# New orders for the attention steps of a transformer block with adaptive layer norms and a mixture of experts

## What is computed

```python
h = _layernorm(x, axis=-1) * (1 + ca) + sa
x = x + ga * _L0_attn_ref(h, ...)   # inner layer norm, k, v, r, running sum over rows, Wo
h = _layernorm(x, axis=-1) * (1 + cb) + sb
x = x + gb * _L0_ffn_ref(h, ...)    # two groups of 32 experts, top 2 of each, SwiGLU
```

## Time and profile before

| what | value |
|---|---|
| time, median of 3 runs | 4911.22 us (4901.27 to 4916.95) |
| time of the profiled execution | 4905.73 us |
| its span | 4904.0 us |
| TensorE busy | 4580.8 us (93%) |
| VectorE busy | 3080.2 us (63%) |
| GpSimd busy | 2858.1 us (58%) |
| ScalarE busy | 1651.2 us (34%) |
| mean granted clock of TensorE | 0.971 |

### The profile page before, as it was taken

One profiled execution on the slowest core, in us unless ns is written; L12 is line 12 of the kernel. 1 busy time (PEld: TensorE's weight loads), 2 busy tenths in 40 slices (PEclk: granted clock), 3 DMA queues, 4 the chain that ended last, 5 costly groups with the idle time before them and its releaser, 6 DMA issues.

```text
span 4904.0 us, 89177 instructions
## 1 busy us (share of the span) xinstructions
PE 4580.8 (93%) x22649; PEld 3764.6 (77%) x22649; DVE 3080.2 (63%) x6077; ACT 1651.2 (34%) x4093; POOL 2858.1 (58%) x2300
## 2 busy tenths in 40 slices
PE   6999999999999995889999998999999999999998
PEld 4877777777777774667777777888788888888887
DVE  5999999999999996444444444444344444444443
ACT  2444444444444442222222222332222222222222
POOL 2577777777777776445444454555455555555554
PEclk8999999999999997899999999999999999999999
DMA  6767666666666674889899989998998988988887
GB/s 240 234 200 228 195 222 196 214 200 220 207 200 227 196 226 159 261 271 285 252 279 280 280 238 270 294 278 223 290 239 222 260 221 242 258 231 221 220 222 195
DMA packets 434624, 1152.46 MB, mean 235 GB/s; under 512 B 59361, under 2 KB 59362, under 8 KB 415666
## 3 DMA queue, kind: packets, MB, share of 16 engines
q0 software_dynamic: 182512, 454.27, 39.3%
q1 hardware_dynamic: 231106, 619.79, 36.6%
q10 hardware_dynamic: 20736, 75.51, 4.2%
HBM read 719.35 MB, written 463.57 MB: 241 GB/s over the span
## 4 chain that ended last, share of the span: by engine, by line
PE 42%; DMA 12%; issue 4%; POOL 2%; DVE 1%; POOLq 0%; SPq 0%; ACT 0%; DVEq 0%
PE ps L1316 12%; PE ps L1318 12%; PE ps L1317 12%; DMA out<-c_yo,c_idx 11%; PE ps L1325 4%; PE ps L1344 2%; POOL out L1307 1%; POOL c_xg L1274 1%; DMA c_wt<-wsp_d 0%; POOLq L1299 0%; DVE c_yo L1571 0%; POOL list_d L1279 0%; DMA list_d<-pairs,sidx 0%; DMA c_lists<-list_d,c_rowu 0%; DVE c_xl L1559 0%
## 5 line engine op out<-in xcount | busy, mean ns | idle before, releaser
L1307 POOL DMA_INDIRECT out<-c_yo,c_idx x576 | 915.1, 1589 | 933.9 <-DMA out<-c_yo,c_idx 512.5
L1316 PE MATMUL ps<-c_wt,c_xh 128*128 128x512 f32 x2304 | 964.1, 418 | 24.9 <-issue 16.8
L1318 PE MATMUL ps<-c_wt,c_xl 128*128 128x512 f32 x2304 | 910.3, 395 | 0.0
L1317 PE MATMUL ps<-c_wt,c_xh 128*128 128x512 f32 x2304 | 904.0, 392 | 0.0
L1274 POOL DMA_INDIRECT c_xg<-h2g_d,c_idx x576 | 565.0, 981 | 507.6 <-DVE c_yo L1571 400.5
L1555 DVE TENSOR_TENSOR c_hh<-ps,c_sil 128x256 f32<-128x256 f32 x576 | 244.2, 424 | 913.5 <-ACT c_sil L1398 843.5
L1571 DVE SCALAR_TENSOR_TENSOR c_yo<-ps,c_wc,c_xg 128x512 f32<-128x512 f32 x576 | 432.3, 750 | 529.2 <-PE ps L1318 261.5
L442 PE MATMUL ps<-xTh,wTh 128*128 128x512 f32 x1536 | 625.9, 407 | 53.5 <-DVE xTl L818 46.9
L1403 ACT CAST c_xh<-ps 128x512 fp32r<-128x512 f32 x576 | 339.2, 589 | 962.2 <-PE ps L1325 874.2
L709 POOL DMA_INDIRECT list_d<-pairs,sidx x496 | 545.5, 1100 | 188.5 <-issue 123.9
L1398 ACT ACTIVATE c_sil<-ps 128x256 f32<-128x256 f32 x576 | 221.3, 384 | 1177.1 <-PE ps L1318 1105.3
(11 more groups left out here) (199 smaller groups left out, 7776.2 us busy)
## 6 DMA issues: line engine op xcount, KB each, us to landing
c_wt<-wsp_d SPq DMA_DIRECT2D x69, 2048.0 KB
sraw<-wex SPq DMA_DIRECT2D x290, 256.0 KB
wsp_d<-shigh SPq DMA_DIRECT2D x288, 256.0 KB
wsp_d<-sraw SPq DMA_DIRECT2D x288, 256.0 KB
c_wt<-wsp_d SPq DMA_DIRECT2D x69, 1024.0 KB
xin<-x SPq DMA_DIRECT2D x34, 1024.0 KB
h2g_d<-mod_d SPq DMA_DIRECT2D x128, 256.0 KB
out<-xin SPq DMA_DIRECT2D x32, 1024.0 KB
```

Source lines behind the costliest of these rows:

```text
L1307: nc.gpsimd.indirect_dma_start(out=out, out_offset=bass.IndirectOffsetOnAxis(ap=idx[:, n:n + 1], axis=0), in_=yo[:, n % 4, :], in_offset=N ...
L1316: nc.tensor.matmul(o, lh, rh, start=first, stop=False)
L1317: nc.tensor.matmul(o, lh, rl, start=False, stop=False)
L1318: return nc.tensor.matmul(o, ll, rh, start=False, stop=last)
```

## The change

The order of work inside a step is new on all five engines. TensorE puts `back` after the k part of chunk 3, and `logits` behind `front`, at the end of the step; the group numbers follow, so that some groups take their bank from other groups than before. ScalarE takes jobs 0 and 1 ahead of chunk 0, `hi` of chunk 0 ahead of `soften`, jobs 4 to 6 earlier, and the logits' copy and job 9 last. GpSimd spreads the last five indirect DMAs over the step's start and moves jobs 7 and 9. VectorE takes chunk 0 ahead of `topk`, job 4 ahead of `modulate`, and jobs 5 and 6 ahead of chunk 1. SyncE issues `store_h2` after the store of job 4 instead of before it. In three places a `tensor_scalar` that adds EPS to the variances becomes a `tensor_reduce` that sums each variance and an EPS kept beside it.

The group numbers, and SyncE's queue:

```diff
-PROJ = ((0, 1, 2), (8, 9, 10), (11, 12, 13), (18, 20, 21))
-OUTP, RANK, BACKT, LOGIT, FRONTT = 3, 7, 14, 19, 22
+PROJ = ((0, 1, 2), (8, 9, 10), (11, 12, 13), (14, 19, 20))
+OUTP, RANK, BACKT, FRONTT, LOGIT = 3, 7, 15, 21, 25
...
                 turn(4)
                 if not (first and s == 0):
                     store_x1(b, s - 1)
+                turn(5)
+                if not (first and s == 0):
                     store_h2(b, s - 1)
...
-                for i in range(5, PER_STEP):
+                for i in range(6, PER_STEP):
                     turn(i)
```

TensorE:

```diff
                 project(b, s, 1)
                 project(b, s, 2)
+                project(b, s, 3, (0,))
                 if not (first and s == 0):
                     back(b, s)
-                project(b, s, 3, (0,))
+                project(b, s, 3, (1, 2))
+                front(b, s)
                 if not (first and s == 0):
                     logits(b, s)
-                project(b, s, 3, (1, 2))
-                front(b, s)
```

ScalarE:

```diff
-                chunk_k(b, s, 0)
                 stage_hi(b, at)
                 stage_hi(b, at + 1)
+                chunk_k(b, s, 0)
                 chunk_r(b, s, 0)
+                hi(b, s, 0)
                 if not (first and s < 2):
                     soften(b, s - 2)
-                hi(b, s, 0)
                 stage_hi(b, at + 2)
                 stage_hi(b, at + 3)
+                stage_hi(b, at + 4)
                 normed(b, s)
-                stage_hi(b, at + 4)
+                stage_hi(b, at + 5)
                 chunk_k(b, s, 1)
-                stage_hi(b, at + 5)
+                stage_hi(b, at + 6)
                 chunk_r(b, s, 1)
                 chunk_k(b, s, 2)
+                hi(b, s, 1)
                 if back_too:
                     turned(b, s)
-                hi(b, s, 1)
-                stage_hi(b, at + 6)
                 chunk_r(b, s, 2)
                 chunk_k(b, s, 3)
                 hi(b, s, 2)
                 stage_hi(b, at + 7)
-                if back_too:
-                    logits(b, s)
                 stage_hi(b, at + 8)
-                stage_hi(b, at + 9)
                 front(b, s, (0, 1))
                 chunk_r(b, s, 3)
                 front(b, s, (2, 3))
                 hi(b, s, 3)
+                if back_too:
+                    logits(b, s)
+                stage_hi(b, at + 9)
```

GpSimd:

```diff
+                stage_lo(b, at)
+                if not (first and s < 3):
+                    scatter(b, s - 3, 11, 13)
                 rstd(f_var, vaf, h_ready, rsf, f_rstd, b, s + 1)
+                stage_lo(b, at + 1)
+                receive(b, s, 0)
                 if not (first and s < 3):
-                    scatter(b, s - 3, 11, 16)
-                stage_lo(b, at)
-                receive(b, s, 0)
-                stage_lo(b, at + 1)
+                    scatter(b, s - 3, 13, 14)
                 lo(b, s, 0)
+                if not (first and s < 3):
+                    scatter(b, s - 3, 14, 16)
+                stage_lo(b, at + 2)
                 rstd(g_var, vag, z_ready, rsg, g_rstd, b, s + 1)
-                stage_lo(b, at + 2)
                 stage_lo(b, at + 3)
...
                 receive(b, s, 2)
-                if old:
-                    scatter(b, s - 2, 8, 9)
+                stage_lo(b, at + 7)
                 lo(b, s, 2)
-                stage_lo(b, at + 7)
                 stage_lo(b, at + 8)
...
-                stage_lo(b, at + 9)
                 receive(b, s, 3)
                 if old:
                     scatter(b, s - 2, 10, 11)
                 lo(b, s, 3)
+                stage_lo(b, at + 9)
```

VectorE (of the three edits of the EPS one is shown, and not the memory of three values a row that they read, nor its filling at the start):

```diff
-                    V.tensor_scalar(vaf[:], mvf[:, :, 1], EPS, None, ALU.add).then_inc(f_var, 1)
+                    V.tensor_reduce(vaf[:], mvf[:, :, 1:3], AX_X, ALU.add).then_inc(f_var, 1)
...
                 norm_front(b, s + 1, 1)
+                chunk(b, s, 0)
                 if not (first and s < 2):
                     topk(b, s - 2)
-                chunk(b, s, 0)
                 norm_front(b, s + 1, 2)
                 if not (first and s == 0):
                     residual(b, s - 1)
                 norm_front(b, s + 1, 3)
                 if not (first and s < 2):
                     place(b, s - 2)
+                stage_lo(b, s * PER_STEP + 4)
                 if not (first and s == 0):
                     modulate(b, s - 1)
-                stage_lo(b, s * PER_STEP + 4)
+                stage_lo(b, s * PER_STEP + 5)
+                stage_lo(b, s * PER_STEP + 6)
                 chunk(b, s, 1)
-                stage_lo(b, s * PER_STEP + 5)
                 chunk(b, s, 2)
-                stage_lo(b, s * PER_STEP + 6)
                 norm_front(b, s + 2, 0)
```

More of the change, by code:

```diff
@@ L284, in worked @@
             if n < 0:
-                return n == -1 and q >= FRONTT
+                return n == -1 and FRONTT <= q < FRONTT + KC
             behind = 2 if q == RANK else 1 if OUTP <= q < RANK or BACKT <= q < BACKT + KC or q == LOGIT else 0
@@ L803, in norm_front @@
                              (g_var, cnt(b, s - 1, 1, 1)), (g_nm, cnt(b, s - 1, 1, 1)))
-                        V.bn_aggr(mvg[:, j, :], stg[:, j, :]).then_inc(g_aggr, 1)
+                        V.bn_aggr(mvg[:, j, 0:2], stg[:, j, :]).then_inc(g_aggr, 1)
                     dve.wait_ge(g_aggr, cnt(b, s, 4, 4))
                     wait(dve, g_rstd, cnt(b, s - 1, 1, 1))
-                    V.tensor_scalar(vag[:], mvg[:, :, 1], EPS, None, ALU.add).then_inc(g_var, 1)
+                    V.tensor_reduce(vag[:], mvg[:, :, 1:3], AX_X, ALU.add).then_inc(g_var, 1)
                 else:
@@ L855, in residual @@
                          (b_var, cnt(b, s - 1, 1, 1)), (h2_half, cnt(b, s - 1, 4, 4)))
-                    V.bn_aggr(mvb[:, j, :], stb[:, j, :]).then_inc(b_aggr, 1)
+                    V.bn_aggr(mvb[:, j, 0:2], stb[:, j, :]).then_inc(b_aggr, 1)
                 dve.wait_ge(b_aggr, cnt(b, s, 4, 4))
                 wait(dve, b_rstd, cnt(b, s - 1, 1, 1))
-                V.tensor_scalar(vab[:], mvb[:, :, 1], EPS, None, ALU.add).then_inc(b_var, 1)
+                V.tensor_reduce(vab[:], mvb[:, :, 1:3], AX_X, ALU.add).then_inc(b_var, 1)
             def modulate(b, s):
@@ L1036, in _ @@
             g.memset(half[:], -0.5)
+            for t in (A["mvf"], A["mvg"], A["mvb"]):
+                g.memset(t[:, :, 2:3], EPS)
             g.memset(hit[:], 0.0)
```

12 lines of the change are left out of this document (6 added, 6 removed).

## The result

| | before | changed |
|---|---|---|
| time, median | 4906.25 us (4901.12 to 4916.95, 4 runs) | 5034.84 us (5030.85 to 5046.68, 4 runs) |
| ratio to before, 95% interval | | 1.0263 (1.0236 to 1.0290) |
| profiled execution, its span | 4905.73, 4904.0 us | 5032.62, 5030.9 us |
| mean granted clock of TensorE | 0.971 | 0.951 |

The change is 2.6% slower, by 129 us. The direction was the forecast's, the size was not: 5035 lies above 4936 and outside 4850 to 5010. It is close to the rival that called the DMA queue the decider (5020).

A forecast was written before the change was run, and what follows sets the result against it. Neither TensorE nor VectorE alone bounds the kernel; they wait for each other in turn. The new chain takes 58.0 us a step against 57.1, 25 us more over 28 steps, giving 4936 us, range 4850 to 5010.

The forecast's parts named there:

- the rival that called the DMA queue the decider: Slower rival: later landing of job 2's and job 4's stores plus TensorE's clock drop, 61 us a step, 5020; chance 0.20.
- the chain: Stage A step: outputs at +20.0, through stores and job 6 to chunk 3's scan at +52.9, next step at 58.0 us.
- The landing: SyncE's queue: job 4's store behind the 1 MB of x lands 8.1 us after the store of x, at +38.6.
- TensorE gets idle time near +42 and before v of chunk 3, both hidden behind VectorE's chain: TensorE late in the step: two idle times said to move at no cost to the step's length.
- The sum: Whole kernel: 0.9 us a step, 25 us over the loop's 28 steps, batch 0's four steps left unchanged; 4936 us.
- `soften`: ScalarE: running after the wait for outputs instead of hidden in it puts 3.95 us on the path, the change's cost.
- gain (1): TensorE at the step's start: `logits` covers the copies and `split_x`, removing a gap worth up to 1.0 to 3.3 us.
- Gain (2): VectorE: fewer collisions with GpSimd at L795 and job 6 free 2.5 and 2.2 us a step.
- Gain (3): VectorE: the 1044 ns `tensor_scalar` becomes a reduction of 0.2 us, freeing some 0.8 us a step; two alike count nothing.
- Faster: the stores are never late: Rival: job 4's store lands by +36, VectorE has no stall, 55.2 us a step, 4858 us; chance 0.27.
- Much faster: Rival: TensorE alone bounds, as `soften` and weight jobs find cover; 52.75 us a step, 4788 us; chance 0.05.
- nothing: Rival: engines wait for each other and slack only changes places, within 15 us of 4911; chance 0.06.

The follow-up runs named there:

- experiment 5: Changed kernel with job 6 moved back on VectorE (behind chunks 1 and 2) and ScalarE (behind the copies of h's transposes): 5028.97 us, 1.0259.
- experiment 3: Changed kernel with `soften` put back ahead of `hi` of chunk 0 on ScalarE: 5019.84 us, 1.0233.
- experiment 14: Changed kernel with the five moves of experiment 8, and group numbers 18 (chunk 3's first group) and 14 to 17 (h's transposes): 4926.27 us, 1.0023.
- experiment 2: Changed kernel with the 1 MB store of x moved behind job 4's store on SyncE's queue: 4959.83 us, 1.0102.
- experiment 12: Changed kernel with two group numbers altered (18 for chunk 3's first group, 14 to 17 for h's transposes): 5027.70 us, 1.0242.
- Experiment 13: Changed kernel with job 6 back on both engines (experiment 5) and the two group numbers of experiment 11: 4931.27 us, 1.0030.
- experiment 7: Kernel before with only TensorE's new order and group numbers, plus the logits' copy and job 9 last, which this forces: 5051.25 us, 1.0309.
- 8: Changed kernel with job 6 back on both engines, x's store behind job 4's, `soften` ahead of `hi`, GpSimd's norm power first: 5070.05 us, 1.0347.
- 9: Changed kernel with TensorE's old order and group numbers, the logits' copy and job 9 as before: 5060.51 us, 1.0302.
- 15: Changed kernel with TensorE's old order and numbers, and job 6 moved back on both engines: 4999.73 us, 1.0175.
- experiment 11: Kernel before with TensorE's new order as in experiment 7, but numbers 18 for chunk 3's first group and 14 to 17 for h's transposes: 4889.41 us, 0.9954.
- 6: Changed kernel with `topk` ahead of chunk 0 on VectorE again: 5024.02 us, 1.0258.

## Why the prediction was wrong

**Up to the middle of the step the chain held** (offsets in the changed step that begins at 1159.82). `hi` of chunk 0 was forecast at +20.0 and came at +19.8 (1179.61); the low part of job 2 was to end at +26.4 and ended at +26.2 (1186.03); `place` was to end at +30.2 and was done when job 4's low part began, at +31.0 (1190.79); the store of x was due at +30.5 and issued at +30.8, that of job 4 at +31.5 against +31.8. VectorE's stall before job 6 was forecast as 2 us and is 3.17.

**The landing was undersized.** Job 6's low part was to be done by +39.9; VectorE went on at 1201.16, +41.3, so 1.4 us are missing. Of these 1.2 are the landing: I took 8.1 us from the store of x to ScalarE's going on, and it was 9.27 (1190.63 to 1199.90). The rest is the store's later issue.

**The step that failed** is the sentence "TensorE gets idle time near +42 and before v of chunk 3, both hidden behind VectorE's chain". The place and the releaser of the idle time were right. Hidden it was not: the clock fell to the 1.2 GHz level behind it. At full clock the 12 transposes take 1.53 us (experiment 5) and not 2.82, and the eleven next gaps between starts are 0.23 us and not 0.43: 3.5 us more. The first 1.3 us, of the transposes, were slack, since v of chunk 3 had to wait for the scan of chunk 2 until 1207.64 in any case. The 2.2 us behind it were not: VectorE's own wait for v of chunk 3, 1.91 us, is what came through. 58.0 plus 1.4 plus 1.9 is 61.3, against 61.1 measured.

The trace of the changed kernel also has steps with the wait and without the slow clock. In the one from 425.35 to 483.63 TensorE waited 3.73 us in `back`, but the clock was high again for v of chunk 3:

```profile
472.33 0.50 PE L444 MATMUL ps<-xTh,wTh 128*128 128x512 f32 x1 [0.76 <-DVE cs L841]
472.66 0.40 PE L445 MATMUL ps<-xTl,wTh 128*128 128x512 f32 x1
```

VectorE didn't wait for it there, and the step took 58.3 us; the one before it, with a wait of 4.06 us and slow matmuls, took 60.9. Three such steps (from 248.40, 306.77 and 425.35) took 57.7 to 58.4 us, which is the forecast's 58. Two more (from 975.11 and 1466.65) are the last of a pass and took 61.7 us, with a wait of 3.1 and 2.3 us at the next step's start.

That TensorE idles could be read in the order; I priced the idle time and left out the clock after it. The Trainium skill (TensorE: Matmul & The Clock Gate, Terms) puts the penalty at the throttled time times the share of the clock withheld; 9.06 us at 0.51 make an estimate of 4.4 us by it, and the rows show 3.5 on TensorE.

**The sum left the first steps alone.** Batch 0's steps and what leads to them took 19.3 us more. Two of these steps have the same wait in `back` (4.30 and 3.83 us), so that it was no case apart. Of the 102 us by which the profiled execution missed the 4931 these are 19; the loop's steps are 82 (106.5 less the 25 forecast), the end 1.

**`soften`** was named as the cost. It is on record as giving up a cover, which is so, but GpSimd's indirect DMAs are a second cover beneath it. Putting it back gave 15 us (experiment 3), and in the kernel of experiment 14 it was back and gave no more than 5 us together with two other moves.

**The gain (1) came**: no wait for `split_x` at the typical step's start. **Gain (2)** came by line but not in sum: VectorE fell from 53.80 to 51.16 us a step, not to 48, for 2.3 us came back at L793, and `nmg` took 1.26 us (1256 ns in the mean of 26) where before it took 160 ns. The 2.5 us that I put on L795 were 0.2 too high: I held its mean duration, 1325 ns, against 0.69 us between starts, where the duration of L868 is 746 ns. **Gain (3)** was 0.88 us for 0.8 forecast; the two instructions like it, which I counted at nothing, gave 0.7 more (617 and 408 ns, now 161 each).

**The rivals.** The slow one had the mechanism and nearly the time: 61 us a step, 5020. It gave 2.5 us to landing and 0.5 to the clock; the rows give 1.4 and 1.9, so that its total is right in part by luck. Job 2's store, to which it gave 4 us, took 2.3 (1186.77 to 1189.03). "Faster: the stores are never late" falls with the 9.27 us. Its counterpart, experiment 2, in which job 4's store is on time, still lies 1% above before. "Much faster" and "nothing" fall with the 61 us a step.

**What makes the loss, as far as shown.** Two stalls stand one behind the other. One is any bank that is released behind job 6: the scan of chunk 1 in the change, the sigmoid of chunk 1 in experiment 12. The other is the bank that the scan of chunk 3 releases, taken by the second group of `front`. In the changed kernel each of the four cases was run: both ties 2.6%, only the first 2.4% (12), only the second 2.6% (5), neither 0.3% (13). So taking one away brings out the other, and only both together show what they cost. In the kernel before the second alone makes 3.1% (7). Two things limit this. Job 6 has a share in the second too, since in experiments 5 and 8 VectorE waits for it on the way to the scan of chunk 3. And in TensorE's old order, where the second tie isn't there, the first explains only part: 3.0% with it (9), 1.75% without (15). The prediction had seen both ties, but summed one path, with both on it, and so could not see that each holds the step without the other.

**Open.** Experiment 13 is still 0.8% behind experiment 11, which has the old orders on the other engines. Three more moves back did not close that (14), so it lies in what remains: on ScalarE and VectorE the places of jobs 0, 1, 4 and 5, of chunk 0, and of `hi` of chunk 1 ahead of the copies of h; the store of h; and most of GpSimd's order, where one indirect DMA more now stands ahead of the product of chunk 1. Apart from chunk 0 on VectorE (6) these weren't tried one by one. Nor is it shown why in the old order of TensorE the rest still costs 1.75% with job 6 moved (15). Its rows show that `back` and `logits` still wait, and from 300 to 1800 us VectorE waits there for TensorE's products for 86.7 us, in the kernel before for 9.4.

## What to carry to other kernels

When groups of results share banks in turn, a new order of the matmuls is also a new table of who waits for whom: write out for each group who releases its bank and when, and try other numbers before giving an order up. Here two numbers decided between 3.1% slower and 0.5% faster with every instruction in the same place. A weight job that waits for a store is best kept from standing ahead of work that frees a bank. If taking a wait away changes nothing, look for the next one behind it before calling it harmless. Price an idle time of TensorE by what runs behind it as well: at the end of the path it cost about double here (4.93 and 4.5 us in experiment 7).

## What the runs showed of the hardware

- The clock fell behind single waits. After 4.56 (the change), 5.66 (9) and 5.32 us (12) matmuls of 512 columns started 0.43 us apart instead of 0.23, and after 4.93 us (7) transposes, `logits` and the next step's first matmuls were slow. It stayed low for 9 us in the change, some 5 us in 9 and 12, and 11.6 us in 7.
- Shorter waits didn't always do it. In experiment 5 the 12 transposes took 1.53 us behind a wait of 2.90 us at 719.72, and 2.82 us behind the same wait at 1624.12. In experiment 13 matmuls behind 2.12 us started 0.23 us apart at 1197.58 and 0.43 at 1490.94. In the change all 22 groups of 12 transposes behind 3.15 to 5.16 us took 2.6 to 2.8 us.
- `logits` took 6.93 us at the low clock and 3.68 at the high one, the 12 transposes 2.82 and 1.53: ratios of 1.9 and 1.8.
- A store of 256 KB let its waiter go on 3.6 us after its last issue; behind a store of 1 MB on the same queue it took 7.7 (experiment 2 and the change).
- Three additions of a constant to four numbers on VectorE took 1044, 617 and 408 ns in the mean before, as a reduction of eight each took 161.
